# A four-layer image network on one core: the hand-ordered instruction streams of five engines laid out anew

## The reference, cut to what matters

```python
x = x + _L0_conv_ref(_gn(x), ...)   # triplet attention: 3 gates from max and mean over an axis, 7x7 convs, softmax mix
x = x + _L1_conv_ref(_gn(x), ...)   # 3x3 convolution, its weight mixed with four circulant projections of itself
x = x + _L2_conv_ref(_gn(x), ...)   # squeeze and excite on a wavelet mean
x = x + _L3_conv_ref(_gn(x), ...)   # shifted window attention, 8x8 windows, 8 heads, relative bias
```

## Time and profile before

| what | before |
|---|---|
| runs, median of 3 | 2741.02 us (2739.1 to 2745.08) |
| the profiled execution, first to last instruction | 2740.3 us |
| its own device time | the page lists none; the median run lies 0.7 us above this span |
| PE / DVE / ACT / POOL busy | 85 / 79 / 56 / 52% |
| granted TensorE clock, mean | 0.951 |
| chain that ended last | PE 54%, DVE 23%, ACT 8% |

### The profile page before, as it was taken

One profiled execution on the slowest core, in us unless ns is written; L12 is line 12 of the kernel. 1 busy time (PEld: TensorE's weight loads), 2 busy tenths in 40 slices (PEclk: granted clock), 3 DMA queues, 4 the chain that ended last, 5 costly groups with the idle time before them and its releaser, 6 DMA issues.

```text
span 2740.3 us, 67622 instructions
## 1 busy us (share of the span) xinstructions
PE 2332.0 (85%) x27766; PEld 1395.9 (51%) x27766; DVE 2165.5 (79%) x3697; ACT 1538.2 (56%) x3566; POOL 1436.9 (52%) x1150
## 2 busy tenths in 40 slices
...
GB/s 155 127 3 16 158 19 18 32 47 171 33 33 47 98 105 33 33 35 174 40 33 39 83 128 33 32 32 161 57 33 25 79 146 33 33 32 57 54 63 41
DMA packets 125428, 176.20 MB, mean 64 GB/s; under 512 B 72496, under 2 KB 114240, under 8 KB 115520
## 3 DMA queue, kind: packets, MB, share of 16 engines
q1 hardware_dynamic: 125120, 171.88, 20.0%
...
## 4 chain that ended last, share of the span: by engine, by line
PE 54%; DVE 23%; ACT 8%; issue 6%; POOL 4%; DMA 2%; SPq 2%; DVEq 0%; POOLq 0%; ACTq 0%
PE F L2082 18%; PE QP L2141 9%; PE QP L2148 4%; PE SP L2173 4%; PE F L1979 3%; PE O L2201 3%; PE QP L2157 3%; PE PTR L2183 2%; PE F L1955 2%; DVE g_raw L1423 2%; DVE xs L1836 2%; DVE mx L1847 1%; ACT xs L1201 1%; POOL tmp L960 1%; DVE sums L1855 1%
## 5 line engine op out<-in xcount | busy, mean ns | idle before, releaser
L2082 PE MATMUL F<-g_raw,cw_hi 128*128 128x512 f16 x2304 | 701.1, 386 | 20.7 <-DVE g_raw L1423 6.5
L1201 ACT ACTIVATE xs<-xs,mx 128x64 f32<-128x64 f32 x1792 | 445.7, 334 | 123.8 <-DVE mx L1847 123.8
L915 POOL TENSOR_TENSOR xs<-xs,rec 128x512 f32<-128x512 f32 x256 | 287.9, 1136 | 432.5 <-DVE rec L1857 428.3
L2082 PE MATMUL F<-g_raw,cw_lo 128*128 128x512 f16 x1152 | 443.8, 385 | 0.0
L2082 PEld LDWEIGHTS F<-g_raw,cw_hi 128*128 128x128 f16 x2304 | 224.2, 99 | 286.5 <-issue 17.8
L1208 ACT ACTIVATE prt<-PTR 128x512 f32<-128x512 f32 x256 | 151.0, 590 | 216.8 <-PE PTR L2183 191.0
L900 POOL TENSOR_TENSOR tmp<-X,uw 128x512 f32<-128x512 f32 x128 | 165.3, 1303 | 164.0 <-DVE y L1709 83.0
L1836 DVE TENSOR_TENSOR xs<-SP,bias 128x1024 f32<-128x1024 f32 (+2 forms) x192 | 159.7, 859 | 100.0 <-issue 54.2
L1423 DVE SCALAR_TENSOR_TENSOR g_raw<-l0c,gn,g_raw 128x512 f16<-128x512 f32 x192 | 171.6, 936 | 72.2 <-ACT g_raw L1140 36.9
L930 POOL TENSOR_TENSOR ot_lo<-ot,ot_hi 128x512 f16<-128x512 f32 x128 | 149.1, 1187 | 145.8 <-ACT ot_hi L1222 132.7
L2141 PE MATMUL QP<-tok_hi,qkv_hi 128*128 128x512 f16 x470 | 180.1, 383 | 43.4 <-ACT qq L1182 17.3
(11 more groups left out here) (331 smaller groups left out, 5586.4 us busy)
## 6 DMA issues: line engine op xcount, KB each, us to landing
...
```

The costliest lines, as they stand in the source:

```text
L915: G.tensor_tensor(keyed(sc[:, u % 4, :]), keyed(sc[:, u % 4, :]), rec[:, u % 4, :].unsqueeze(2).to_broadcast([P, 8, TOK]), ALU.mult).then_ ...
L1201: last = S.activation(keys, keys, ACT.Exp, bias=mx[:, u % 4, i:i + 1])
L2082: last = T.matmul(F[:, n % 2, :], wgt[:, ci, C3 * comp + dx, P * co:P * co + P], win[which], start=(ci == 0 and dx == 0 and j == 0), stop= ...
```

## The change

Only the four tables change. Every stream has the same pieces in the same order as before; what changes is behind which step of M each is issued, and how many are done ahead. The letters in LAST_ROWS are the same in number on each engine but SP, where one L and one S have moved from there to image 0. The core of the diff: FIRST of SP, POOL, DVE and PE; TURN of POOL and PE, with the end of DVE's; AHEAD; the first line of PE's last rows. ACT's tables and TURN of SP are changed in the same manner.

```diff
 FIRST = {
-    "SP": {"norm0a": "Y", "reduce9": "YY", "hwmean1": "Y", "hwmean7": "Z", "mix": "F", "gate7": "Z", "conv1.1": "F",
-        "conv3.1": "F", "conv6.1": "G", "conv12.0": "ZZ", "conv21.1": "F", "conv23.1": "L"},
-    "POOL": {"load": "RRRY", "norm0a": "RRRR", "norm0b": "RY", "reduce4": "R", "reduce5": "R", "reduce10": "RR",
-        "reduce11": "RR", "reduce14": "R", "zpool": "RR", "hwgate": "R", "band1": "R", "bandturn": "R",
-        "hwmean2": "RRRR", "hwmean4": "R", "hwmean6": "RRR", "conv2.0": "DD", "conv2.1": "D", "conv3.0": "DY",
-        "conv6.0": "W", "conv6.1": "W", "conv7.0": "D", "conv7.1": "W", "conv8.1": "D", "conv9.1": "W",
-        "conv11.1": "W", "conv13.1": "W", "conv15.1": "W", "conv17.0": "WW", "conv18.0": "W", "conv19.0": "W",
-        "conv22.1": "W", "conv23.0": "WWWWRR", "conv23.1": "RRRRRRRRRRERRR", "convend": "RRRRRRRERRRRRR"},
...
-    "DVE": {"load": "CCUCYCCCYCCUCYCYUYYUCYUCCCCCYY", "norm0b": "UY", "norm0c": "YY", "reduce0": "Y",
-        "reduce1": "YY", "reduce2": "Y", "reduce3": "Y", "reduce4": "Y", "reduce5": "U", "reduce6": "U",
-        "reduce8": "U", "reduce9": "UUY", "reduce10": "U", "reduce14": "U", "reduce15": "UUYU", "band2": "YY",
-        "bandcopy": "YY", "logits": "YY", "mix": "Y", "mixturn": "Y", "gate0": "Y", "gate6": "Y", "norm1b": "Y",
-        "conv2.0": "B", "conv4.1": "Y", "conv6.0": "J", "conv7.0": "B", "conv7.1": "JB", "conv8.0": "BBJV",
-        "conv9.0": "V", "conv9.1": "VBBYV", "conv10.1": "B", "conv11.0": "VB", "conv11.1": "B", "conv12.0": "Y",
-        "conv13.0": "YY", "conv13.1": "JVBBJ", "conv14.1": "JVV", "conv16.1": "BVU", "conv17.0": "CUVC",
-        "conv18.0": "VVJVJ", "conv19.0": "VVUJV", "conv21.1": "VVV", "conv22.0": "V", "conv22.1": "YUVC",
-        "conv23.1": "UVV", "convend": "JJVJVCCVCVCVVCUVVVCEUUUCEEUECECUEUUEUUCCECUCE"},
-    "PE": {"reduce10": "YY", "hwconv": "Y", "hwmean0": "Y", "hwmean5": "Y", "gate5": "Y", "gate8": "Y",
-        "conv19.1": "Y", "conv23.1": "EEEEEE"},
+    "SP": {"load": "Y", "reduce0": "Y", "hwgate": "Y", "bandcopy": "Y", "hwmean3": "Z", "mixturn": "Z",
+        "gate14": "S", "norm1a": "F", "norm1c": "F", "conv0.0": "G", "conv2.1": "F", "conv3.0": "Z", "conv8.1": "F",
+        "conv12.0": "Z", "conv13.0": "L", "conv14.0": "L"},
+    "POOL": {"load": "R", "norm0a": "RRRYRRR", "reduce0": "R", "reduce1": "RR", "reduce2": "RRYRR", "reduce5": "R",
+        "reduce7": "R", "reduce9": "R", "reduce10": "R", "reduce11": "R", "reduce14": "RR", "reduce15": "RR",
+        "zpool": "R", "band0": "R", "hwmean1": "R", "hwmean2": "RR", "lift3": "D", "conv1.0": "D", "conv1.1": "D",
+        "conv3.0": "D", "conv5.0": "W", "conv8.1": "DD", "conv10.1": "WY", "conv14.1": "WW", "conv15.0": "W",
+        "conv16.1": "WW", "conv17.0": "W", "conv17.1": "W", "conv18.0": "W", "conv19.1": "W", "conv21.1": "W",
+        "conv23.0": "WWWWRRRRRRRR", "conv23.1": "RR", "convend": "RRRRERRRRRRRR"},
+    "ACT": {"load": "YYY", "norm0c": "Y", "reduce0": "Y", "reduce6": "Y", "reduce9": "Y", "zpool": "Y",
...
+    "DVE": {"load": "CCUCCCCCYCCCCCCCCYUCYYYYYYUY", "norm0a": "U", "norm0b": "Y", "norm0c": "YUYY", "reduce0": "Y",
+        "reduce1": "Y", "reduce2": "Y", "reduce3": "Y", "reduce4": "Y", "reduce5": "U", "reduce6": "U",
+        "reduce7": "U", "reduce8": "U", "reduce9": "U", "reduce10": "U", "reduce11": "U", "reduce12": "UY",
+        "reduce13": "U", "reduce14": "U", "reduce15": "YU", "hwrows": "Y", "band0": "Y", "band3": "YY",
+        "logits": "YY", "mix": "Y", "gate0": "Y", "gate8": "Y", "gate12": "Y", "lift1": "Y", "conv3.0": "B",
+        "conv5.1": "BB", "conv6.0": "Y", "conv7.0": "JJ", "conv7.1": "BB", "conv8.1": "J", "conv9.0": "V",
+        "conv9.1": "VVB", "conv10.0": "B", "conv12.0": "BV", "conv12.1": "B", "conv13.0": "VVVB", "conv13.1": "JJ",
+        "conv14.0": "BV", "conv14.1": "J", "conv15.1": "V", "conv16.0": "B", "conv16.1": "BV", "conv17.0": "V",
+        "conv18.0": "JVU", "conv18.1": "V", "conv19.0": "VCVJ", "conv19.1": "JU", "conv20.1": "VVVV",
+        "conv21.0": "U", "conv21.1": "VVVY", "conv22.1": "U", "conv23.1": "VV",
+        "convend": "JJJVCVVVVVVVCUUCCYUCUCACCUCEUCYEEUEUEECCCYECCYUEE"},
+    "PE": {"reduce13": "Y", "zpool": "YY", "hwmean7": "Y", "logits": "Y", "gate4": "Y", "norm1c": "Y",
+        "convend": "EEEEEEY"},
...
 TURN = {
-    "POOL": {"norm0a": "RRERR", "norm0b": "NR", "norm0c": "N", "reduce3": "RR", "reduce4": "RR", "reduce7": "R",
-        "reduce8": "NR", "reduce10": "R", "reduce13": "RNR", "reduce15": "RRRRR", "zpool": "ORRNRRR", "hwgate": "N",
-        "band0": "NRRN", "band1": "RR", "band2": "O", "bandturn": "N", "hwmean0": "NN", "hwmean1": "N", "mix": "O",
-        "gate0": "NNN", "gate6": "N", "gate13": "O", "gate17": "N", "norm1a": "NN", "lift1": "N", "conv0.0": "O",
-        "conv1.0": "DN", "conv4.0": "D", "conv5.0": "NN", "conv5.1": "D", "conv6.0": "WDWWD", "conv7.1": "NW",
-        "conv9.1": "D", "conv10.0": "NN", "conv11.0": "ON", "conv11.1": "WW", "conv14.0": "N", "conv18.0": "WW",
-        "conv18.1": "W", "conv19.0": "OW", "conv19.1": "WNN", "conv21.1": "WN", "conv23.0": "NWWWW",
-        "conv23.1": "EO"},
...
-        "conv18.1": "JJVV", "conv19.0": "VVTS", "conv19.1": "V", "conv20.0": "V", "conv20.1": "CC",
-        "conv21.0": "UTCCUCV", "conv21.1": "V", "conv22.0": "KAK", "conv23.0": "VCA",
-        "convend": "JJJVVVVCVVVVVEECEECESCECESE"},
...
-    "PE": {"norm0b": "Q", "norm0c": "QT", "reduce0": "TQ", "reduce1": "QW", "reduce3": "Q", "reduce4": "T",
-        "reduce5": "QW", "reduce6": "SWT", "reduce7": "QS", "reduce8": "WQ", "reduce12": "Q", "reduce13": "T",
-        "reduce14": "Q", "reduce15": "Q", "hwconv": "QW", "hwgate": "TQTWQTWQW", "hwrows": "SQSQ", "band3": "Q",
-        "hwmean0": "Q", "hwmean3": "QTQ", "hwmean5": "Q", "hwmean6": "TW", "hwmean7": "TSWTW", "mix": "QWSQ",
-        "mixturn": "Q", "gate0": "T", "gate1": "Q", "gate3": "Q", "gate5": "QT", "gate6": "Q", "gate7": "TQ",
-        "gate8": "WSW", "gate9": "TSWW", "gate11": "Q", "gate12": "Q", "gate13": "Q", "gate16": "Q",
-        "gate17": "QQQT", "norm1a": "QT", "lift0": "SWT", "lift1": "WQ", "lift3": "STWWQ", "conv0.1": "Q",
-        "conv1.0": "Q", "conv2.1": "T", "conv6.1": "Q", "conv7.0": "Q", "conv7.1": "QT", "conv8.0": "Q",
-        "conv8.1": "WTWS", "conv9.1": "Q", "conv10.0": "T", "conv10.1": "SWW", "conv12.0": "Q", "conv12.1": "Q",
-        "conv13.1": "QT", "conv14.0": "Q", "conv15.0": "WQT", "conv15.1": "T", "conv16.0": "QT", "conv16.1": "WWQ",
-        "conv17.0": "QWS", "conv18.0": "S", "conv19.1": "Q", "conv22.1": "Q", "conv23.0": "Q",
-        "conv23.1": "TQTWWTQWQTEWE", "convend": "QEESEQSEQ"},
...
+    "POOL": {"norm0a": "RRERRRR", "reduce0": "NNRR", "reduce3": "R", "reduce4": "RRNR", "reduce5": "R",
+        "reduce10": "RRNRR", "reduce11": "R", "reduce13": "R", "reduce14": "RR", "hwconv": "RORNNR", "band3": "R",
+        "bandcopy": "R", "hwmean0": "RN", "hwmean1": "RNO", "hwmean3": "N", "hwmean5": "NN", "logits": "N",
+        "gate3": "O", "gate4": "N", "gate8": "NN", "gate9": "N", "gate15": "ONN", "gate17": "N", "norm1b": "N",
+        "lift3": "OD", "conv3.1": "D", "conv5.0": "D", "conv5.1": "NWN", "conv6.1": "DW", "conv7.1": "W",
+        "conv9.1": "D", "conv10.0": "N", "conv10.1": "D", "conv11.0": "N", "conv11.1": "WN", "conv12.0": "WO",
+        "conv12.1": "W", "conv13.0": "N", "conv16.0": "WW", "conv17.0": "N", "conv17.1": "W", "conv18.1": "NW",
+        "conv19.1": "W", "conv20.0": "WO", "conv23.1": "NNNNWW", "convend": "WWEO"},
...
+        "conv15.1": "BBVVCVC", "conv16.0": "VBVAV", "conv16.1": "VKAK", "conv17.0": "UV", "conv18.0": "TJCJCCU",
+        "conv19.0": "JVV", "conv19.1": "VCVCV", "conv20.0": "VSCV", "conv20.1": "S", "conv21.1": "CVCC",
+        "conv22.0": "TU", "conv22.1": "ATC", "conv23.0": "K", "conv23.1": "CCKA", "convend": "JJJCVVVVVVVVEECEEESEESE"},
...
+    "PE": {"norm0a": "Q", "norm0b": "QTQ", "reduce0": "Q", "reduce2": "Q", "reduce3": "T", "reduce4": "Q",
+        "reduce6": "WW", "reduce7": "ST", "reduce8": "STQ", "reduce9": "WW", "reduce10": "Q", "reduce13": "Q",
+        "reduce14": "Q", "reduce15": "TQ", "hwconv": "QWTQTWQWTQ", "hwgate": "WS", "hwrows": "Q", "band0": "S",
+        "band1": "Q", "band3": "Q", "hwmean0": "T", "hwmean1": "Q", "hwmean2": "TW", "hwmean3": "Q",
+        "hwmean5": "QTW", "hwmean7": "QTWWS", "logits": "SQ", "mix": "Q", "mixturn": "Q", "gate1": "Q", "gate3": "Q",
+        "gate4": "TQ", "gate5": "TQ", "gate7": "Q", "gate8": "WST", "gate9": "WT", "gate10": "WSW", "gate11": "Q",
+        "gate12": "Q", "gate13": "Q", "gate14": "Q", "gate15": "QQ", "gate16": "TQ", "norm1a": "Q", "norm1b": "T",
+        "lift0": "ST", "lift2": "WW", "lift3": "TWQWQ", "conv0.0": "Q", "conv1.1": "SQ", "conv5.1": "Q",
+        "conv6.0": "Q", "conv6.1": "T", "conv8.0": "T", "conv8.1": "Q", "conv9.1": "Q", "conv10.0": "S",
+        "conv10.1": "TW", "conv11.0": "W", "conv12.1": "ST", "conv13.1": "Q", "conv14.0": "WW", "conv15.0": "QT",
```

(7 more changed lines are left out.)

13 lines of the change are left out of this document (7 added, 6 removed), and 54 rows, old and new, of tables (FIRST, TURN).

## The result

| kernel | median us (range, runs) | ratio to before, 95% interval |
|---|---|---|
| before | 2741.7 (2739.1 to 2745.1, 4) | |
| after | 2755.7 (2751.4 to 2758.3, 4) | 1.0048 [1.0034, 1.0063] |

The change makes the kernel 0.5% slower, where I had forecast 1.0% faster. The profiled execution of after spans 2753.8 us, 13.5 more than the one of before. A line number of after is that of before plus 2: L1494 there is L1496 here.

A forecast was written before the change was run, and what follows sets the result against it. PE was taken to bound the periods, DVE and POOL with their order both ends of the first image. Terms -9 -4 -6 +3 -10.5 = -26.5 on the span 2740.3 gave 2713.8, median 2714.5 us; range 2688 to 2744.

The forecast's parts named there:

- Term 1: First image up to zpool: -9 us, from shorter waits on weights, scratch_w and POOL's sums, less slower DVE additions.
- Term 2: First image, 141 to 217 us: no change, ends -3 and +3; low5 at lift1 costs only its own 2 us.
- Term 3: Convolution of image 0: -4 us, from moving POOL's two all-reduces behind conv10.1 and DVE setup out; ends -10 and 0.
- term 4: 331 to 389 us, up to image 1's group norm: -6 us, as 22 of POOL's 28 R are done ahead; ends -9 and -3.
- Term 5: Image 1's period: +3 us given back, as six R and three U return to it; ends 0 and +8.
- Term 6: Seven fronts with attention: -1.5 us each, -10.5 in all; ends -4 and +2 per front.
- about -2: Gates of each front: about -2 us, as the projections standing in a row at gate17 are spread behind gate14 to gate16.
- about -1: End of each period: about -1 us, as DVE's last string before group norm has two C instead of five.
- +1.5, a guess from its 0.1 us of slack: Convolution of each front: +1.5 us, since it had no idle time and can only get some.
- rival C: Slower kernel: shifted attention pieces on PE, DVE and ACT make holes in each period's convolution; 2760 at 5 us net per front; 14%.
- Term 7: The last rows: no change, ends -4 and +4.
- Rival B: The clock stays up once the gate burst of waits is gone, 20 us more over seven periods, 2694; 11%.

The follow-up runs named there:

- f2: After with several later edits, among them the first image's two POOL all-reduces moved to conv5.0 and DVE's low5 back to norm1b; 2713.2 us, 0.9892 of before.
- x1_first: Cross of both kernels: first-image tables (FIRST, AHEAD) from after, later tables (TURN, LAST_ROWS) from before; 2730.4 us, 0.9956 of before.
- n2: On m1_nnw, POOL's four normalisings (N) moved from conv23.1 to conv22.1, ahead of its last sum; 2723.3 us, 0.9927 of before.
- k_cnq: On m1_nnw, three DVE statistics (C) moved behind L1401, ACT's q1 reading ahead of the second T, normalisings' move without effect; 2742.9 us, 1.0003 of before.
- m1_nnw: After with one POOL letter moved: behind conv5.1 both normalisings ahead of the weighted row (NNW for NWN); 2729.8 us, 0.9961 of before.
- k_s: On m1_nnw, the second group of scores moved from conv20.1 to conv21.0 on PE and DVE; 2731.9 us, 0.9952 of before.
- k_n: Meant to move POOL's normalisings on m1_nnw, but left its order unchanged, so a repeat of it; 2736.0 us, 0.9958 of before.

## Why the prediction was wrong, point by point

**Term 1 (-9): right.** The step s3 (PE's L2002), just behind zpool and the 3D gate, starts 9.7 us earlier on PE. (a) DVE's wait on the weights' DMA fell from 11.2 to 7.6 us, -3.6 for -4.2. (b) PE's wait on scratch_w is gone. (c) So is DVE's 4.3 on POOL's sums. Its moved setup and the additions beside the sums (some now over 2.2 us) were paid in the reduce steps, where PE waited 15.1 us in one piece for DVE.

**Term 2 (0): wrong, +10.5.** PE began the first convolution at 218.4 us, 0.8 later than before, with 9.7 in hand at s3. Of the 10.5, 4.2 were lost up to the mean of the second norm and 6.3 from there to the convolution. I can name 7.5 of them. One low piece ran beside POOL and took 2.17 + 2.55 us for 1.23 + 0.68; I had taken every low at its price without POOL. And low5 at lift1 does hold up PE, which waited 11.2 us there for 6.5 in before, though f2 shows that at most 1.4 us of it counted.

**Term 3 (-4) and term 4 (-6): sizes right.** From the first convolution's start to its end 108.2 us for 113.1, -4.9; from there to image 1's marker 50.6 for 58.6, -8.0. But term 3's way was wrong, and its size is luck. PE's 4.8 at conv11 went, and a wait of 7.8 came at conv16, behind the block's new place, as its upper end had it. The stretch is shorter because PE entered it late: its wait of 3.97 on L1494, there in before, had already been waited for ahead of the convolution, under term 2. f2 shows the exchange: with low5 back PE enters 6.5 us earlier, waits 4.34 on L1496, and the first image is 1.4 us shorter.

**Term 5 (+3): right way, a third of the size.** Image 1 took 306.4 us in x1_first for 305.4 in before.

**Term 6 (-1.5 per front): the step that failed.** It came at about +4 per front: images 1 to 6 together are 25.8 us longer, of which 1.0 is term 5's. What failed is the part for the convolution, and behind it the order on POOL. Its three parts, as means of images 1 to 6:
- "about -2" at gate17: right in size, and more than half by luck. PE's idle time from gate8 to the convolution fell by 2.3 us (8.0 to 5.7), the clock stayed up, and the stretch is 3.7 us shorter (some work moved out of it as well). The waits of the four projections fell only from 3.6 to 2.4 us in image 3; they still follow one another every 2.34 us. The wait for the values, which I had said stays, fell from 2.97 to 1.36:
```profile
1143.04 0.28 PE L2150 MATMUL QP<-qkv_hi,tok_hi 128*128 128x256 f16 x1 [1.36 <-ACT vv L1191]
```
  And all this was worth little. From PE's mean of the second norm to the first take-out L1496 DVE and ACT need 26.4 us in after and 27.3 in before (L1494); PE enters the convolution 3.7 us earlier after gate8, and 0.9 is left of it. What I had not asked is who is late next when PE gets there sooner.
- "about -1" behind the convolution: +1.6 in length. I counted DVE's statistics against PE's wait of 2.03, and that wait is 2.03 in after as well. The four N that now stand behind conv23.1 slow DVE's joined rows by 2.1 us (n2); moving three more statistics away brought L1401 no earlier (k_cnq). The granted clock of the stretch also fell, from 0.97 to 0.92.
- "+1.5, a guess from its 0.1 us of slack": the convolution became 8.2 us longer, and PE's idle time in it rose by 5.9 us (0.8 to 6.6). Of them 1.9 came by one N behind a W on POOL (m1_nnw), about 1 by stalls within score groups whose cause is open (k_s), some 3 as the gates' gain given back. The rows of before held the warning: a stretch with almost no idle time, into whose order many pieces were dealt anew.

I had looked for rival C's hole in ACT's and DVE's lists. The one that decided the sign came from POOL's: an engine busy 52% of the time, on which I followed the order of R and Y, but not N against W. With that letter moved, the kernel is 0.4% faster than before.

**Term 7 (0): right.** From the last matmul of the last convolution to the end it is 211.6 us for 211.0. **Rival B**, the clock: half right. The low stretch behind the gate burst is gone in all periods (0.96 to 1.00 above, and no low clock in any gate stretch of images 1 to 6), as the Trainium skill, "TensorE: Matmul & The Clock Gate", section "HAM oscillation — how this bites in real kernels", would have it. Other places have more of it. PE's busy time at the lower clock, in images 1 to 6, fell from 12.7 us to none in the gates, but rose from 10.0 to 23.3 at the end of the periods; over the whole span it is 165 us in before and 166 in after. Two executions of one order differ by 20 us in this sum (m1_nnw, k_n), so that the totals are equal says little. And the price that B put on the gates, 20 us, was high: 12.7 us there and 13.3 in the convolution behind them are worth 13 us at half speed over six periods.

The range ended at 2744 and missed by 12 us. C had 14% and a price of 2 to 5 us net per front; it came at 4. Of the signs that the prediction named for being wrong, the first marker (377.2 us, under 380) did not show it; the periods, which moved by 4.0 us where 3 was the limit, did. The forecast for the first image, -19, came at -12.1.
